# Two gated MLP layers in a one-core Trainium2 kernel: token shift by transfers, 11 column blocks, four banks, bias as a row

## The chip, the core and the metric

The kernel runs on one NeuronCore of one Trainium2 chip. The metric is the device time of one execution in microseconds (us). A core has TensorE (PE in the profile; its weight loads are PEld), VectorE (DVE), ScalarE (ACT), GpSimd (POOL), SyncE (SP, which here only issues transfers) and 16 DMA engines.

## The reference, cut to what matters

The input is x, 4096 tokens of 256 channels. First comes global causal attention with 16 heads, whose result is kept for the end. Then come DEPTH = 2 layers, each a local attention and a gated MLP, and at last a gate that puts the two paths together. The change touches the gated MLP alone:

```python
DIM = 256; HID = int(DIM * 4 * 2 / 3)      # 682
def shift_token(t):                         # half of the channels come from the token before
    t1, t2 = jnp.split(t, 2, axis=-1)
    t2 = jnp.pad(t2, ((0, 0), (1, 0), (0, 0)))[:, :-1]
    return jnp.concatenate([t1, t2], axis=-1)
...
h = shift_token(x)
mu = h.mean(-1, keepdims=True)
var = h.var(-1, keepdims=True)
h = (h - mu) / jnp.sqrt(var + 1e-05) * lg + lb
h = h @ w1 + b1                             # 256 -> 2 * 682
a, g = jnp.split(h, 2, axis=-1)
h = a * jax.nn.gelu(g, approximate=False)
x = x + h @ w2 + b2                         # 682 -> 256
```

## The kernel before, in words

The stages run one after the other with a barrier between them: `project`, `global_attention`, `project_out`, then twice `local_attention_layer` and `mlp_layer`, and `gate`. X, the residual stream, stays on the chip as X[128 tokens, 32 tiles, 256 channels].

`mlp_layer` (L1406) handles the 4096 tokens in NC = 8 chunks of 512 (TPC = 4 tiles of 128). Each float32 product is made of three fp32r ones (`product3`, L72): each operand is split in a high part, rounded, and a low part, the rest. Before the first chunk there is a preparation: SP loads w1 into `stage` (L1468) and six small tensors (L1470); ACT rounds w1 (L1500), DVE subtracts (L1582); then SP loads w2 into the same `stage` (L1474), and ACT and DVE do the same with it. ACT and PE also wait for the small tensors.

Then each engine runs the function `slot(k)` for k = 0 to 8. In slot k the front half works on chunk k (shift, statistics, normalisation, turning) and the back half on chunk c = k - 1 (up projection, gate, down projection). Slot 0 has only a front half, slot 8 only a back half; slots 1 to 7 are iterations of a loop. Within a slot each engine has a fixed order:

- PE: the shift (L1535, L1537), eight matmuls in float32 by a shift matrix and a carry matrix into `bank_sh`; the up projection (L1554 to L1557), 12 column blocks of 128, of which each takes 6 matmuls of 512 columns (two halves of the channels, three products); the turning of the normalised chunk k, 8 transposes (L1563); the down projection (L1572), 72 matmuls of 256 columns into `bank_y`, the first tile of which waits for each split of u in turn (`ul_done`).
- The blocks of the up projection alternate between a gate block (n even) and an up block (n odd) and use UR = 3 banks of PSUM in turn: block n >= 3 waits until the reader of block n - 3 is done (L1549), which is Gelu on ACT (L1514) for a gate block and the product on DVE (L1621) for an up block.
- DVE, all of the front half first: bn_stats of the half of the channels that stays (L1590) and of the shifted half in PSUM (L1593), bn_aggr (L1598), epsilon (L1600), the normalisation in eight pieces (L1604, L1606); then X + b2 into `xb` (L1611); then for each of HC = 6 pairs of blocks the product (up + bias) * gelu (L1621) and its rounding (L1627); then the split of the turned chunk (L1634, L1637); at last X = bank_y + xb (L1645).
- ACT: six Gelu (L1514), then scale and bias of the turned chunk (L1520). POOL: the power -1/2 for the normalisation (L1485), then six low parts of u (L1493).

Three transfers of other stages are read below for their rate: `kst<-gone` (L554) copies 128 runs of 512 B from 128 partitions into 2 partitions, `oraw<-o_raw` (L802) reads an array whose outermost dimension is 4 into 64 partitions, and `y_rows<-oy` (L806) has 128 partitions on both sides. An `xs` transfer of the shifted half is 127 partitions x 4 runs of 512 B.

HID is 682 = 5 * 128 + 42, so that the sixth pair of blocks holds 42 columns of use in each block of 128; the rest are zeros.

Of the kernel before, what the change touches and what calls it, by code (L numbers as in the profile page):

```python
# [41 lines left out]
HP = HC * P  # L42

# [1362 lines left out]
def mlp_layer(nc, layer, X, w_1, w_2, b_1, ln_cols, b_2, ident, shift, carry):  # L1406


    with ExitStack() as ctx:
# [5 lines left out]
        def psum(name, shape):  # L1415
# [5 lines left out]
        b1_sb = sb("b1", [P, 2 * HC])  # L1421
        ln_sb = sb("ln", [P, 2 * EC])
        b2_sb = sb("b2", [P, E])
        id_sb = sb("id", [P, P])
        sh_sb = sb("sh", [P, P])
        ca_sb = sb("ca", [P, P])
        half = sb("half", [P, TPC])
        stats = sb("stats", [P, TPC, 2, 6])
# [10 lines left out]
        xb = sb("xb", [P, TPC, E])  # L1439
        bank_sh = psum("bank_sh", [P, TPC, P])  # L1440
        bank_t = psum("bank_t", [P, EC, C])
        UR = 3
# [5 lines left out]
        names = ("sh", "st", "ag", "ve", "rs", "hn", "th", "hf", "hhi", "hlo", "um", "gl", "uf", "uh", "ul", "y", "xb", "x3")  # L1448
        (sh_done, st_done, ag_done, ve_done, rs_done, hn_done, th_done, hf_done, hhi_done, hlo_done, um_done,
         gl_done, uf_done, uh_done, ul_done, y_done, xb_done, x3_done) = [sem(n) for n in names]  # L1450
# [10 lines left out]
        def tile(k, a):  # L1461
            return X[:, bass.ds(k * TPC + a, 1), :]
# [3 lines left out]
        @block.sync  # L1466
        def _(sp):
            sp.dma_start(stage[:, :], w_1).then_inc(w1_in, 16)  # L1468
            for dst, src in ((b1_sb, b_1), (ln_sb, ln_cols), (b2_sb, b_2), (id_sb, ident), (sh_sb, shift), (ca_sb, carry)):
                sp.dma_start(dst[:, :], src).then_inc(const_in, 16)  # L1470

            sp.wait_ge(wh_done, 1)
            sp.wait_ge(wl_done, 1)
            sp.dma_start(stage[:, 0:HC * E], w_2).then_inc(w2_in, 16)  # L1474

        @block.gpsimd
        def _(pool):
# [3 lines left out]
            def slot(k):  # L1481
                if live(k):
                    pool.wait_ge(ve_done, k + 1)
                    upto(pool, hn_done, 2 * TPC * k)
                    pool.tensor_tensor(rstd[:, :], ve[:, :], half[:, :], ALU.pow).then_inc(rs_done, 1)  # L1485
                if live(k - 1):
                    c = k - 1
                    for m in range(HC):
# [4 lines left out]
                        pool.tensor_tensor(u_lo[:, m, :], uf[:, m % 2, :], u_hi[:, m, :].bitcast(F32), ALU.subtract  # L1493
                                           ).then_inc(ul_done, 1)
            slots(pool, slot)

        @block.scalar
        def _(act):
# [4 lines left out]
            act.wait_ge(const_in, 6 * 16)  # L1503

            def slot(k):
                if live(k - 1):
                    c = k - 1
                    for m in range(HC):
                        act.wait_ge(um_done, 2 * (c * HC + m) + 1)
# [4 lines left out]
                        act.activation(gl[:, m % 2, :], bank_u[(2 * m) % UR][:, :], ACT.Gelu,  # L1514
                                       bias=b1_sb[:, HC + m:HC + m + 1]).then_inc(gl_done, 1)
# [9 lines left out]
        def _(pe):  # L1525
            pe.wait_ge(const_in, 6 * 16)
# [3 lines left out]
            def slot(k):  # L1530
                if live(k):
                    upto(pe, hn_done, 2 * TPC * k)
                    for a in range(TPC):
                        first = isinstance(k, int) and k == 0 and a == 0
                        last = pe.matmul(bank_sh[:, a, :], sh_sb[:, :], tile(k, a)[:, :, P:E], start=True, stop=first)  # L1535
                        if not first:
                            last = pe.matmul(bank_sh[:, a, :], ca_sb[:, :], tile(k, a - 1)[:, :, P:E], start=False, stop=True)  # L1537
                    last.then_inc(sh_done, 1)
                c = k - 1
                if live(c):  # L1540
                    pe.wait_ge(hlo_done, c * EC + EC)
                    pe.wait_ge(hhi_done, c * EC + EC)
                    for m in range(HC):
                        for side in range(2):
                            n = 2 * m + side

                            if n >= UR:
                                mm, ss = (n - UR) // 2, (n - UR) % 2
                                pe.wait_ge(uf_done if ss else gl_done, c * HC + mm + 1)  # L1549
                            elif n == 0:  # L1550
                                upto(pe, uf_done, c * HC)
                                upto(pe, gl_done, c * HC)
                            col = (HP if side == 0 else 0) + m * P
                            for e in range(EC):  # L1554
                                last = product3(pe, bank_u[n % UR][:, :], w1_hi[:, e, col:col + P], w1_lo[:, e, col:col + P],
                                                h_hi[:, e, :], h_lo[:, e, :], e == 0, e == EC - 1)
                            last.then_inc(um_done, 1)  # L1557
                if live(k):
                    pe.wait_ge(hn_done, 2 * TPC * (k + 1))
# [5 lines left out]
                if live(c):  # L1565
                    upto(pe, x3_done, c * TPC)
                    for a in range(TPC):
                        for m in range(HC):
                            if a == 0:
                                pe.wait_ge(ul_done, c * HC + m + 1)  # L1570
                            tok = slice(a * P, (a + 1) * P)
                            last = product3(pe, bank_y[:, a, :], u_hi[:, m, tok], u_lo[:, m, tok], w2_hi[:, m, :],  # L1572
                                            w2_lo[:, m, :], m == 0, m == HC - 1)
# [5 lines left out]
        def _(dve):  # L1579
# [219 lines left out]
```

## Time and profile before

| | |
|---|---|
| median of 3 runs | 3534.86 us (3532.56 to 3538.28) |
| profiled execution: its time / its span | 3537.87 us / 3536.2 us |
| PE busy, share of the span | 3162.5 us, 89% |
| DVE busy | 2373.5 us, 67% |
| ACT busy | 1722.9 us, 49% |
| POOL busy | 785.7 us, 22% |
| mean granted TensorE clock | 0.954 |
| gated layer 0, from the load of w1 to the last X | 2338.4 to 2613.9 us of the span |
| gated layer 1, the last X | 3499.0 us |

Busy shares are averages over stages with different limits. The two gated layers take some 275 us each, and what an edit in them is worth is to be read there, from what each engine waits for in one slot.

### The profile page before, as it was taken

What the parts mean: (1) busy time and instruction counts of PE and PEld (TensorE: products, weight loads), DVE (VectorE), ACT (ScalarE), POOL (GpSimd) and SP (SyncE); (2) the same over time, 40 slices, a digit from 0 to 9 for tenths busy, and PEclk for the clock granted to TensorE, in tenths of its full rate; (3) what the DMA queues carried; (4) which work ended last, traced back from release to release, by engine and by line L of the source; (5) the groups of instructions that cost most, each with busy time, mean ns of one, the idle gap of its engine ahead of it and who ended that gap; (6) DMA issues with size and microseconds to landing.
All of it is one profiled execution on the core that took longest, in us unless ns stands there. A gap on an engine that the chain in (4) does not pass through costs nothing. (4 is left out here: it accounts for less than half of the span.)

```text
span 3536.2 us, 76024 instructions
## 1 busy us (share of the span) xinstructions
PE 3162.5 (89%) x31852; PEld 1928.2 (55%) x31852; DVE 2373.5 (67%) x3284; ACT 1722.9 (49%) x3173; POOL 785.7 (22%) x757
## 2 busy tenths in 40 slices
PE   7799999999999999998689999959968999995995
PEld 6433333344443433343467777647856777764784
DVE  7699998987899988772356555535535655553554
ACT  4267777887678888886033333222213333322221
POOL 7400000000110000001043333312224333331221
PEclk9699999999999999997899999979989999997998
DMA  7420001000210000000300000000010000000004
GB/s 242 130 61 17 9 9 45 9 14 13 59 39 9 13 13 5 5 8 23 127 24 14 20 20 14 8 32 0 0 34 24 14 20 20 14 8 32 0 0 143
DMA packets 62014, 113.62 MB, mean 32 GB/s; under 512 B 9608, under 2 KB 25480, under 8 KB 61192
## 3 DMA queue, kind: packets, MB, share of 16 engines
q1 hardware_dynamic: 57608, 102.84, 9.5%
q10 hardware_dynamic: 4096, 6.30, 0.7%
q8 instruction: 237, 3.88, 0.5%
q14 instruction: 73, 0.60, 0.1%
HBM read 74.77 MB, written 33.55 MB: 31 GB/s over the span
## 5 line engine op out<-in xcount | busy, mean ns | idle before, releaser
L649 DVE TENSOR_REDUCE mp<-ps_m 128x2 f32<-128x1024 f32 (+3 forms) x1152 | 1275.7, 1135 | 186.2 <-PE ps_m L700 132.9
L627 ACT ACTIVATE probs<-ps_s 128x512 f32<-128x512 f32 (+3 forms) x2304 | 1162.6, 561 | 372.8 <-PE ps_s L724 342.2
L740 PE MATMUL ps_o<-probs,vall 128*32 128x256 f32 (+3 forms) x9216 | 708.4, 379 | 15.7 <-POOL probs L604 9.1
L724 PE MATMUL ps_s<-qst,kst 64*128 64x512 f32 (+3 forms) x2304 | 593.0, 484 | 4.5 <-ACT probs L627 3.1
L700 PE MATMUL ps_m<-kst,qst 64*128 64x512 f32 (+3 forms) x2304 | 479.1, 399 | 33.4 <-DVE mp L649 15.8
L724 PEld LDWEIGHTS ps_s<-qst,kst 64*128 64x128 f32 x2304 | 240.7, 186 | 457.2 <-ACT probs L627 399.3
L740 PEld LDWEIGHTS ps_o<-probs,vall 128*32 128x32 f32 x9216 | 185.5, 109 | 339.8 <-issue 175.3
L700 PEld LDWEIGHTS ps_m<-kst,qst 64*128 64x128 f32 x2304 | 231.8, 191 | 78.0 <-DVE mp L649 58.7
L989 POOL TENSOR_TENSOR a_rot<-a_t 128x512 f32<-128x512 f32 x128 | 163.0, 1273 | 448.6 <-DVE a_t L1344 448.6
L1514 ACT ACTIVATE m_gl<-m_bank_u,m_b 128x512 f32<-128x512 f32 x96 | 66.3, 691 | 344.4 <-PE m_bank_u L77 344.4
L1035 ACT ACTIVATE a_sq<-a_BP 128x512 f32<-128x512 f32 x128 | 76.6, 599 | 292.8 <-PE a_BP L77 292.8
L604 POOL TENSOR_SCALAR_AFFINE_SELECT probs<-probs 128x256 f32<-128x256 f32 x256 | 103.2, 408 | 509.0 <-ACT probs L627 508.9
L1344 DVE SCALAR_TENSOR_TENSOR a_t<-a_BP,a_sc,a_tab 128x256 f32<-128x256 f32 x384 | 167.1, 476 | 63.5 <-ACT a_sq L1035 63.0
L593 POOL TENSOR_TENSOR msplit<-negm,mzero 128x16 fp32r<-128x16 f32 x32 | 7.2, 224 | 903.4 <-DVE negm L655 903.4
L995 POOL TENSOR_TENSOR a_rn<-a_ssc,a_half 128x32 f32<-128x32 f32 x32 | 174.1, 5440 | 94.1 <-DVE a_ssc L1401 94.1
L1042 ACT ACTIVATE a_oTh<-a_on 128x512 fp32r<-128x512 f32 x64 | 40.4, 631 | 296.6 <-DVE a_on L1354 296.6
L75 PE MATMUL m_bank_u<-m_hh,m_w1h 128*128 128x512 f32 x384 | 155.6, 405 | 27.8 <-DVE m_uf L1621 27.8
L1350 DVE RECIPROCAL a_rec<-a_B 128x256 f32<-128x256 f32 x64 | 112.3, 1754 | 100.0 <-PE a_B L1213 99.5
L1014 ACT ACTIVATE a_PT<-a_SU 128x1024 f32<-128x1024 f32 (+1 forms) x128 | 122.3, 1007 | 108.9 <-PE a_SU L1135 108.9
L1317 DVE TENSOR_REDUCE a_mx<-a_SU 128x4 f32<-128x1024 f32 (+1 forms) x128 | 148.6, 1203 | 39.1 <-PE a_SU L1111 39.1
L1493 POOL TENSOR_TENSOR m_ul<-m_uf,m_uh 128x512 fp32r<-128x512 f32 x96 | 126.2, 1315 | 193.8 <-DVE m_uh L1627 193.8
L76 PE MATMUL m_bank_u<-m_hl,m_w1h 128*128 128x512 f32 x384 | 152.4, 397 | 0.0
(182 smaller groups left out, 5271.3 us busy)
## 6 DMA issues: line engine op xcount, KB each, us to landing
a_tab<-in_rope SPq DMA_DIRECT2D x32, 512.0 KB
q_parts<-pparts SPq DMA_DIRECT2D x32, 256.0 KB, 3.9
k_parts<-pparts SPq DMA_DIRECT2D x32, 256.0 KB, 3.9
qst<-q_parts SPq DMA_DIRECT2D x64, 128.0 KB, 2.6
o_raw<-o_sb SPq DMA_DIRECT2D x32, 256.0 KB, 2.1
X<-in_x SPq DMA_DIRECT2D x8, 512.0 KB, 6.1
kst<-k_parts SPq DMA_DIRECT2D x32, 128.0 KB, 3.7
qst<-q_parts SPq DMA_DIRECT2D x64, 64.0 KB, 2.6
```

The source lines that it names most:

```text
L75: pe.matmul(out, a_hi, b_hi, start=start, stop=False)
L76: pe.matmul(out, a_hi, b_lo, start=False, stop=False)
L627: act.activation(probs[:, s % PR, h, off:C], sslots[n % SR][:, off:C], ACT.Exp, scale=float(D) ** -0.5).then_inc(exp_done, 1)
L649: dve.tensor_reduce(mp[b % 2][:, h:h + 2, cc:cc + 1], slot[:, :, 0:width], AX.X, ALU.max).then_inc(max_read, 1)
L700: last = pe.matmul(slot[:, x, 0:width], qst[q_slot(b)][rows, hp, a * P:(a + 1) * P], kst[g % 2][rows, hp, cc * C:cc * C + width], start=Tr ...
L724: pe.matmul(sslots[n % SR][:, off:C], kst[g % 2][rows, hp, i * P:(i + 1) * P], qst[q_slot(b)][rows, hp, off:C], start=True, stop=True).the ...
L740: last = pe.matmul(ps_o[32 * h:32 * h + VW, lo:hi], vall[:, i, (g * GH + h) * DV:(g * GH + h) * DV + VW], probs[:, s % PR, h, lo:hi], star ...
L989: pool.tensor_tensor(rot[:, g, :, :].rearrange("p a b -> p (a b)"), t[:, n % 2, 0, :, :].rearrange("p a b -> p (a b)"), t[:, n % 2, 1, :, ...
L995: pool.tensor_tensor(rn[:, :, :, :].rearrange("p a b c -> p (a b c)"), ssc[:, :, :, :].rearrange("p a b c -> p (a b c)"), half[:, :], ALU. ...
L1317: dve.tensor_reduce(mx[:, w % 2, 2 * b:2 * b + 2, :], SU[:, 2 * b:2 * b + 2, :].rearrange("p i (q c) -> p i q c", q=2)[:, :, :, lo:N2], AX ...
L1344: dve.scalar_tensor_tensor(out=dst, in0=src, scalar=s, in1=table, op0=ALU.mult, op1=ALU.mult).then_inc(rope_done, 1)
L1493: pool.tensor_tensor(u_lo[:, m, :], uf[:, m % 2, :], u_hi[:, m, :].bitcast(F32), ALU.subtract).then_inc(ul_done, 1)
```

## The change

- The shift matmuls, their bank, and the two matrices go. SP copies chunk k into a new tile `xs` by three transfers inside SBUF: the half that stays (128 partitions), the shifted half (partitions 0 to 126 to partitions 1 to 127), and row 0 from partition 127 of the tile before. It issues those of chunk 0 between the loads of w1 and of the small tensors, those of chunk k >= 1 when chunk k - 1 is normalised. bn_stats and the normalisation read `xs`, 256 channels at a time.
- The weights w1 are laid out as NB = 11 blocks: gate and up alternate for five pairs, and the last block holds both remainders, up columns in rows 0 to 41 and gate columns in rows 64 to 105. The last Gelu and the last product both wait for it.
- `bank_u` has four banks in place of three.
- b2 becomes row 42 of the last block of w2, against a row of ones in u; `xb` goes, and X = bank_y + X is done in two pieces of 512 in place of four. The last block of the down projection uses 64 rows.
- DVE no longer does the front half ahead of the gate: bn_stats follows the first product, bn_aggr the second, the normalisation the third and the fourth (two tiles each). POOL does the power after its second low part.

```diff
-        UR = 3
+        UR = 4
...
+        def shifted(sp, k):
+            t = k * TPC
+            sp.dma_start(xs[:, :, 0:P], X[:, t:t + TPC, 0:P]).then_inc(xs_in, 16)
+            sp.dma_start(xs[1:P, :, P:E], X[0:P - 1, t:t + TPC, P:E]).then_inc(xs_in, 16)
+            if k == 0:
+                sp.wait_ge(one_set, 1)
+                sp.dma_start(xs[0:1, 1:TPC, P:E], X[P - 1:P, 0:TPC - 1, P:E]).then_inc(xs_in, 16)
+            else:
+                sp.dma_start(xs[0:1, :, P:E], X[P - 1:P, t - 1:t + TPC - 1, P:E]).then_inc(xs_in, 16)
...
             sp.dma_start(stage[:, :], w_1).then_inc(w1_in, 16)
-            for dst, src in ((b1_sb, b_1), (ln_sb, ln_cols), (b2_sb, b_2), (id_sb, ident), (sh_sb, shift), (ca_sb, carry)):
+            shifted(sp, 0)
+            for dst, src in ((b1_sb, b_1), (ln_sb, ln_cols), (id_sb, ident)):
                 sp.dma_start(dst[:, :], src).then_inc(const_in, 16)
 
             sp.wait_ge(wh_done, 1)
             sp.wait_ge(wl_done, 1)
             sp.dma_start(stage[:, 0:HC * E], w_2).then_inc(w2_in, 16)
+
+            for k in range(1, NC):
+                sp.wait_ge(hn_done, TPC * k)
+                shifted(sp, k)
...
+                    if live(k) and m == 1:
+                        pool.wait_ge(ve_done, k + 1)
+                        upto(pool, hn_done, TPC * k)
+                        pool.tensor_tensor(rstd[:, :], ve[:, :], half[:, :], ALU.pow).then_inc(rs_done, 1)
...
+                        n, r = block_of(m, 0), gate_rows(m)
+                        act.activation(gl[uses(m), m % 2, :], bank_u[n % UR][r, :], ACT.Gelu,
+                                       bias=b1_sb[r, n:n + 1]).then_inc(gl_done, 1)
...
-                if live(k):
-                    upto(pe, hn_done, 2 * TPC * k)
-                    for a in range(TPC):
-                        first = isinstance(k, int) and k == 0 and a == 0
-                        last = pe.matmul(bank_sh[:, a, :], sh_sb[:, :], tile(k, a)[:, :, P:E], start=True, stop=first)
-                        if not first:
-                            last = pe.matmul(bank_sh[:, a, :], ca_sb[:, :], tile(k, a - 1)[:, :, P:E], start=False, stop=True)
-                    last.then_inc(sh_done, 1)
...
+                    for n in range(NB):
+                        if n >= UR:
+                            pe.wait_ge(uf_done if n % 2 else gl_done, c * HC + (n - UR) // 2 + 1)
...
+            def gated(c, m):
+                n, r, b = c * HC + m, uses(m), block_of(m, 1)
+                dve.wait_ge(um_done, c * NB + b + 1)
+                dve.wait_ge(gl_done, n + 1)
...
+                dve.scalar_tensor_tensor(out=uf[r, m % 2, :], in0=bank_u[b % UR][r, :], scalar=b1_sb[r, b:b + 1],
+                                         in1=gl[r, m % 2, :], op0=ALU.add, op1=ALU.mult).then_inc(uf_done, 1)
+                dve.wait_ge(uf_done, n + 1)
...
+                dve.tensor_copy(u_hi[r, m, :], uf[r, m % 2, :]).then_inc(uh_done, 1)
+
+            def measure(k):
+                dve.wait_ge(xs_in, 48 * (k + 1))
+                for a in range(TPC):
+                    dve.bn_stats(stats[:, a, :], xs[:, a, :]).then_inc(st_done, 1)
...
+            def normalize(k, a):
+                if a == 0:
+                    dve.wait_ge(rs_done, k + 1)
+                    upto(dve, th_done, k * EC)
+                dve.tensor_scalar(hn[:, a, :], xs[:, a, :], mv[:, a, 0:1], rstd[:, a:a + 1], ALU.subtract, ALU.mult
+                                  ).then_inc(hn_done, 1)
...
+                for m in range(HC):
+                    if live(c):
+                        gated(c, m)
+                    if live(k):
                         if m == 0:
+                            measure(k)
+                        elif m == 1:
+                            aggregate(k)
+                        elif m in (2, 3):
+                            normalize(k, 2 * m - 4)
+                            normalize(k, 2 * m - 3)
...
-                    for a in range(TPC):
-                        dve.tensor_tensor(tile(c, a).rearrange("p a e -> p (a e)"), bank_y[:, a, :], xb[:, a, :], ALU.add
-                                          ).then_inc(x3_done, 1)
+                    for a in range(0, TPC, 2):
+                        x = X[:, bass.ds(c * TPC + a, 2), :]
+                        dve.tensor_tensor(x, bank_y[:, a:a + 2, :], x, ALU.add).then_inc(x3_done, 1)
```

## Rows read from the trace of the kernel before

**Rows 1.** Stretches: us, then each engine's busy time, granted clock, DMA share, GB/s.

```profile
2432.10:2463.00 30.90, 28.48 (x170) 24.62 (x170) 17.61 (x46) 6.88 (x9) 8.91 (x7) 1.00 0.00 0
```

**Rows 2.** Timeline, DVE, X written at a slot's end: start, us, instruction, idle before.

```profile
2401.71 1.42 DVE L1645 TENSOR_TENSOR X<-m_bank_y,m_xb 128x256 f32 x4 [5.34 <-PE m_bank_y L77]
...
2586.32 1.42 DVE L1645 TENSOR_TENSOR X<-m_bank_y,m_xb 128x256 f32 x4 [5.58 <-PE m_bank_y L77]
2612.51 1.42 DVE L1645 TENSOR_TENSOR X<-m_bank_y,m_xb 128x256 f32<-128x256 f32 x4 [8.17 <-PE m_bank_y L77]
...
3285.37 1.42 DVE L1645 TENSOR_TENSOR X<-m_bank_y,m_xb 128x256 f32 x4 [5.58 <-PE m_bank_y L77]
3317.49 1.42 DVE L1645 TENSOR_TENSOR X<-m_bank_y,m_xb 128x256 f32 x4 [5.34 <-PE m_bank_y L77]
```

**Rows 3.** Timeline, PE, one slot of layer 0.

```profile
2432.16 0.38 PE L1535 MATMUL m_bank_sh<-X,m_sh 128*128 x2
...
2433.86 0.48 PE L75 MATMUL m_bank_u<-m_hh,m_w1h 128*128 128x512 f32 x1
...
2439.30 0.40 PE L77 MATMUL m_bank_u<-m_hh,m_w1l 128*128 128x512 f32 x1
2441.76 0.50 PE L75 MATMUL m_bank_u<-m_hh,m_w1h 128*128 128x512 f32 x1 [2.06 <-DVE m_uf L1621]
...
2453.07 1.04 PE L1563 MATMUL m_bank_t<-m_id,m_hn 128*128 128x128 f32 x8
...
2455.59 0.28 PE L77 MATMUL m_bank_y<-m_w2h,m_ul 128*128 128x256 f32 x1
2456.24 0.38 PE L75 MATMUL m_bank_y<-m_w2h,m_uh 128*128 128x256 f32 x1 [0.36 <-POOL m_ul L1493]
```

**Rows 4.** Timeline, DVE, ACT and POOL, the same slot.

```profile
2439.62 1.42 DVE L1611 TENSOR_TENSOR m_xb<-X,m_b 128x256 f32<-128x256 f32 x4
...
2442.86 0.96 DVE L1627 CAST m_uh<-m_uf 128x512 fp32r<-128x512 f32 x1
...
2451.86 0.69 ACT L1514 ACTIVATE m_gl<-m_bank_u,m_b 128x512 f32<-128x512 f32 x1 [2.11 <-PE m_bank_u L77]
...
2453.42 0.75 DVE L1621 SCALAR_TENSOR_TENSOR m_uf<-m_bank_u,m_b,m_gl 128x512 f32<-128x512 f32 x1 [1.59 <-PE m_bank_u L77]
...
2454.72 1.46 POOL L1493 TENSOR_TENSOR m_ul<-m_uf,m_uh 128x512 fp32r<-128x512 f32 x1 [1.52 <-DVE m_uh L1627]
```

**Rows 5.** Timeline, preparation, slot 0 and start of slot 1 of layer 0.

```profile
2351.29 0.33 SPq L1474 DMA_DIRECT2D m_stage<-in_w  x1
2355.76 1.48 ACT L1502 ACTIVATE m_w2h<-m_stage 128x1536 fp32r<-128x1536 f32 x1 [7.93 <-DMA m_stage<-in_w]
...
2362.54 0.89 DVE L1593 BATCH_NORM_STATS2 m_stats<-m_bank_sh 128x6 f32<-128x128 f32 x4 [2.73 <-PE m_bank_sh L1537]
...
2367.74 1.97 PE L1563 MATMUL m_bank_t<-m_id,m_hn 128*128 128x128 f32 x8 [5.24 <-DVE m_hn L1606]
...
2372.78 0.61 PE L75 MATMUL m_bank_u<-m_hh,m_w1h 128*128 128x512 f32 x1
```

**Rows 6.** Timeline, DVE, the first stage: bn_stats of four tiles of 256 channels.

```profile
4.89 1.41 DVE L323 BATCH_NORM_STATS2 pstats<-X 128x6 f32<-128x256 f32 x4 [4.89 <-DMA X<-in_x]
```

**Rows 7.** Stretches, columns as in rows 1: kst<-gone; oraw<-o_raw; a stretch with y_rows<-oy.

```profile
242.00:242.50 0.50, 0.41 (x4) 0.10 (x4) 0.50 (x2) 0.17 (x2) 0.00 (x0) 1.00 0.14 43
1695.00:1705.00 10.00, 10.00 (x40) 7.38 (x39) 4.83 (x8) 0.00 (x0) 0.00 (x0) 1.00 0.26 102
1713.00:1717.00 4.00, 4.00 (x16) 2.85 (x15) 1.56 (x3) 0.00 (x0) 0.00 (x0) 1.00 1.03 413
```

**Rows 8.** Timeline, SP's queue: the issue of the transfer in the first stretch of rows 7.

```profile
240.17 1.14 SPq L554 DMA_DIRECT2D kst<-gone  x2
```

**Rows 9.** DMA issues: tile, queue, count, KB each, median us to landing.

```profile
m_b<-in_b SPq DMA_DIRECT2D x2, 128.0 KB, 5.5
...
obo<-in_b_o SPq DMA_DIRECT2D x1, 128.0 KB, 2.6
```

More of the change, by code:

```diff
@@ L1403, in _, with mlp_layer @@
                 divide(k - 3, 0)
-def mlp_layer(nc, layer, X, w_1, w_2, b_1, ln_cols, b_2, ident, shift, carry):
+def mlp_layer(nc, layer, X, w_1, w_2, b_1, ln_cols, ident):
     with ExitStack() as ctx:
@@ L1481, in slot @@
             def slot(k):
-                if live(k):
[L1483 to L1488, printed above, removed]
+                c = k - 1
+                for m in range(HC):
+                    if live(c):
                         pool.wait_ge(uh_done, c * HC + m + 1)
@@ L1542, in slot @@
                     pe.wait_ge(hhi_done, c * EC + EC)
[L1543 to L1557, printed above, removed]
+                    for n in range(NB):
+                        if n >= UR:
+                            pe.wait_ge(uf_done if n % 2 else gl_done, c * HC + (n - UR) // 2 + 1)
+                        elif n == 0:
+                            upto(pe, uf_done, c * HC)
+                            upto(pe, gl_done, c * HC)
+                        col = slice(n * P, (n + 1) * P)
+                        for e in range(EC):
+                            last = product3(pe, bank_u[n % UR][:, :], w1_hi[:, e, col], w1_lo[:, e, col],
+                                            h_hi[:, e, :], h_lo[:, e, :], e == 0, e == EC - 1)
+                        last.then_inc(um_done, 1)
                 if live(k):
-                    pe.wait_ge(hn_done, 2 * TPC * (k + 1))
+                    pe.wait_ge(hn_done, TPC * (k + 1))
                     upto(pe, hf_done, k * EC)
@@ new lines, in measure, with aggregate @@
+            def measure(k):
+                dve.wait_ge(xs_in, 48 * (k + 1))
+                for a in range(TPC):
+                    dve.bn_stats(stats[:, a, :], xs[:, a, :]).then_inc(st_done, 1)
+            def aggregate(k):
+                dve.wait_ge(st_done, TPC * (k + 1))
+                dve.memset(idle[:, :], 0.0)
+                for a in range(TPC):
+                    dve.bn_aggr(mv[:, a, :], stats[:, a, :]).then_inc(ag_done, 1)
+                dve.wait_ge(ag_done, TPC * (k + 1))
+                dve.tensor_scalar(ve[:, :], mv[:, :, 1], EPS, None, ALU.add).then_inc(ve_done, 1)
@@ L1628, in slot @@
+                for m in range(HC):
+                    if live(c):
+                        gated(c, m)
+                    if live(k):
+                        if m == 0:
+                            measure(k)
[4 more added lines that the diff above has]
+                            normalize(k, 2 * m - 3)
                 if live(k):
@@ L1640, in slot @@
                     dve.wait_ge(y_done, c + 1)
-                    dve.wait_ge(xb_done, TPC * (c + 1))
-                    upto(dve, sh_done, (k + 1) if not isinstance(k, int) else min(k + 1, NC))
-                    for a in range(TPC):
-                        dve.tensor_tensor(tile(c, a).rearrange("p a e -> p (a e)"), bank_y[:, a, :], xb[:, a, :], ALU.add
-                                          ).then_inc(x3_done, 1)
+                    for a in range(0, TPC, 2):
+                        x = X[:, bass.ds(c * TPC + a, 2), :]
+                        dve.tensor_tensor(x, bank_y[:, a:a + 2, :], x, ALU.add).then_inc(x3_done, 1)
             slots(dve, slot)
```

118 lines of the change are left out of this document (49 added, 69 removed).

## The prediction, made before the changed kernel was run

> **What bounds the kernel now.** The change is confined to the two gated layers, so I read a gated slot. The stretches give granted clock 1.00, PE busy 28.5 of 30.9 us and DVE 17.6 [rows 1]: PE bounds it. The writes of X mark the slots: six full slots of layer 0 take (2586.32 - 2401.71) / 6 = 30.77 us each, the last 26.2, slot 1, from the turning at 2367.74 to the write at 2401.71, some 34.0 [rows 2, 5]. PE's timeline divides a slot [rows 3]: shift 2432.16 to 2433.86 = 1.70 us; four blocks in 5.67, of which the last matmul starts at 2439.30; then a hole until 2441.76, which at one matmul each 0.233 us is 2.22 us; eight blocks in 11.3 to 2453.07 (1.40 us a block); turning, 0.8; 15 down matmuls; 2455.59 to 2456.24, where one matmul needs 0.12, is 0.53 lost to the last low part of POOL; the rest of the down projection. The hole is of DVE's order: block 4 waits for the first product, which stands behind the whole front half and `xb` (to 2441.0) [rows 4].
>
> **The change part by part, per steady slot.**
>
> - *Shift matmuls* go: -1.70 [rows 3]. Nothing hides them, PE being the bound.
> - *Eleven blocks for twelve*: one block, -1.40. The down projection stays at 72 matmuls; 64 rows in place of 128 I cost at nothing (bounds 0 and, if a matmul went by its rows, 12 x 0.12 / 2 = -0.7).
> - *The hole*: -2.22. The first product now stands first in its slot. It waits only for block 1, 2.8 us in, and takes 0.75 [rows 4]; block 5 wants its bank at 7.0, block 4 that of the first Gelu, done at about 2.3. The four banks give a block of room more. What is late next is the front half, below.
> - *The last pair*: Gelu of the last block ran beside the last up block; now it follows it. The chain block, (Gelu 0.69), product 0.75, rounding, low part 1.46 [rows 4] grows by Gelu and a handover, 0.69 + 0.05. PE waits there already, so all of it shows: +0.74, and the wait becomes about 1.27. Bounds: 0.5 if the smaller partition count makes something shorter, 1.5 if DVE is late by one piece of normalisation.
> - *The front half in the gaps.* Products come each 2.8 us and need 0.75 + 0.43, so each gap has 1.6. bn_stats of four tiles of 256 took 1.41 [rows 6], bn_aggr and epsilon some 0.8, two normalisations some 0.8: each fits its gap. POOL: the second low part ends 8.3 us in, the power at 9.3, the normalisation starts at 9.8 and ends, undisturbed, at 13.4; the turning wants it at 15.4. Cost 0. If this cover of 2 us is gone, each us late is one us per slot.
> - *DVE and POOL*: a rounding that began while POOL worked took 0.96 in place of 0.43 [rows 4], that is, it waited. The normalisation of tiles 2 and 3 now begins just as POOL begins the fourth low part (1.29); if it waits too, it ends at 14.7, still ahead of 15.4. The Trainium skill (SBUF — State Buffer, "SBUF: two separate sides") says that the loser of the shared port blocks for the whole instruction; by that rule the 14.7 is the figure to hold against the trace, and the sum is the same.
> - *`xb`* goes and the last sum is two pieces for four: DVE has room, and PE's wait for it (`x3_done`) lies a slot away. 0.
> - *SP and the transfers.* SP has nothing else in these layers. The doubtful one is the shifted half: 508 runs of 512 B on 127 partitions. In the rows, two partitions on one side ran at 43 GB/s, an outermost dimension of four at 102, 128 at 413 [rows 7]: 21.5, 25.5 and 25.8 GB/s for each of 2, 4, 16 DMA engines, as if the outermost dimension were dealt out evenly. 127 can't be dealt out evenly but to one. Bounds: 260 KB over 16 engines, under 1 us plus latency; over one, 260 KB / 21.5 = 12.1 us. I take one engine, the nearest rule to the rows. With 2.1 us before the first packet (two issues of about 0.5; the packets of a copy issued at 240.17 fill the stretch from 242.00 [rows 7, 8]) it lands 14.2 us after the last normalisation. That is 13.4 + 14.2 = 27.6; the next slot's bn_stats come at 26.2 + 4.2 = 30.4. Hidden, with 2.8 us to spare, 1.5 if POOL delays the normalisation. The Trainium skill (DMA: Bandwidth & Descriptors, "Why a DMA increments its semaphore by 16 and not by 1") says the same of 127 partitions: one engine.
>
> Per steady slot: -1.70 - 1.40 - 2.22 + 0.74 = -4.58, to 26.2 us. Six per layer: -27.5.
>
> **Preparation and slot 0.** Here the long transfer isn't hidden. It is issued behind w1 and ahead of w2, and a queue's later transfers wait: 128 KB landed 5.5 us after its issue behind w1, 2.6 elsewhere [rows 9]. w1 ends at about 2345; one engine then works 0.8 + 12.1 us on `xs`, to 2357.9, and only then on its sixteenth of w2 (48 KB, 1.9 us): 2359.8 in place of 2355.76 [rows 5], +4.1. Against it: DVE's wait of 2.73 for the shift goes [rows 5], bn_stats take 1.41 where two halves took 1.76, the normalisation four pieces for eight, about -0.75: -3.8. Sum +0.3 a layer. Bounds: -3.8 if 16 engines share it, +1 if w1 suffers too.
>
> **Slot 1.** The blocks began at 2372.78; DVE's split lets them begin 0.5 sooner, but at half clock: the turning at 2367.74 took 1.97 us where a warm one takes 1.04 [rows 3, 5], and the shift matmuls that ran until the clock rose are gone. A matmul of 512 columns at 1.2 GHz is 0.43 for 0.23; some 5 us of it, as long as turning and shift took before the rise, cost 2.3. The first `xs` of the loop lands 14.2 us after the normalisation of chunk 0, bn_stats wait for it (3 us), and the whole front half runs late, so that the last product and the turning just meet it. Blocks end at about 22.2, u is complete at 25.8, the down projection ends at 32.6 us, where it was 33.8: -1.2. Bounds -3.5 and +1.5.
>
> **Slot 8**: one block less, the longer last pair: -1.40 + 0.74 = -0.7.
>
> Per layer 0.3 - 1.2 - 27.5 - 0.7 = -29.1; two layers -58.2. In layer 1 slot 2 took 32.1 in place of 30.8 [rows 2]; the clock fell after a hole of 2 us. With holes of 1.3 I expect it not to: -1.3. Sum **-59.5 us**, against the profiled execution (3537.87, span 3536.2, so 1.7 around it) 3478.4; that execution is 3.0 above the median 3534.86, so **3475 us**.
>
> **The rivals.**
>
> - *A. Sixteen engines share the shifted half.* For it: 512 runs would divide, and no row has 127. Against: rows 7 as read. Then preparation and slot 0 give -3.8 in place of +0.3, slot 1 about -0.2 more: 2 x 4.3 = 8.6, 3467 us.
> - *B. The front half or the last pair is late.* Two registers more to wait for and the lock between DVE and POOL let the turning wait, or u ends a further 1 to 1.5 us late, or the clock falls in the new waits. For it: 0.7 us of cover by the locked figure. 14 slots x 1.3 = +18: 3493 us.
> - *C. Slower than before: the transfer sets the pace.* Then the period is landing time plus the way from bn_stats to the last normalisation (1.4 + 1.2 + POOL's low part and power 2.4, two normalisations, a product, two more: 7.8 us). It decides at 26.2 when landing takes 18.4, and loses to 30.77 at 23, which is 41 ns a run of 512 B for the 23.8 of rows 7. Were it 60 ns, as with crowded engines, the landing is 32.6, the period 40.4: 14 x 9.6 + preparation 2 x 18 = +170, some 3705 us. Against: in these stretches DMA share is 0.00 [rows 1], nothing crowds it.
> - *D. The change doesn't do what it says*: the banks or the order don't free block 4, the hole stays, 14 x 2.2 back: 3506 us.
>
> **How the numbers follow.** A measurement of this kernel tells about 0.2% (7 us) from no change. Forecast 0.6, A 0.16, B 0.13, C 0.05, D 0.04, and 0.02 for a mixture of B and C that ends within 7 us of before. Forecast, A, B and D are faster by more than that, C is slower. The range takes in A below, with slot 1 at its good end, and B above with the upper bound of the last pair: 3460 to 3500. Faster 0.93, same 0.02, slower 0.05.
>
> **What would show it.** In the changed profile: no L75 matmul of block 4 idle behind a product; slots of 26.2 us; PE idle some 1.0 to 1.3 before the sixth split of u; a gap between the loads of w2 and its rounding of 8.5 us in place of 4.5; bn_stats waiting for `xs` in slot 1 only; the first blocks of slot 1 at half clock. Wrong if: slots are equal to landing time plus 8 (C); w2 lands in 4.5 us (A); the turning waits for DVE in each slot (B).

## The result, and the profile after

| | us, median (lowest to highest) | ratio to before, 95% interval |
|---|---|---|
| before | 3535.69 (3531.43 to 3541.13), 6 runs | |
| after | 3520.51 (3511.63 to 3522.59), 6 runs | 0.9954 [0.994, 0.9968] |

Faster by 15 us (0.5%) where 60 were forecast, and outside the range of 3460 to 3500. The profiled execution took 3522.59, with a span of 3520.9.

So that noise elsewhere in the kernel stays out, I cut each gated layer by its own marks, the issue of w1, the turning of chunk 0, and the writes of X, and add the two layers. Forecast is the row of before with the prediction's terms.

| both gated layers, us | before | forecast | after |
|---|---|---|---|
| w1's issue to the turning | 58.4 | 59.0 | 62.6 |
| slot 1, from the turning | 68.2 | 65.8 | 82.9 |
| slots 2 to 7 | 370.4 | 314.1 | 331.8 |
| slot 8 | 52.6 | 51.2 | 55.5 |
| sum | 549.6 | 490.1 | 532.8 |

The rest of the kernel took 2986.6 and 2988.1. Of the 42.7 us that are missing, 17.1 lie in slot 1, 17.7 in the slots that repeat, 3.6 in the preparation and 4.3 in slot 8. The slots that repeat come first. In the timeline of VectorE of the kernel after, the writes of X at the ends of slots 2, 3 and 4 of layer 0 (against [rows 2]):

```profile
2440.83 1.29 DVE L1666 TENSOR_TENSOR X<-m_bank_y,X 128x512 f32 x2 [6.84 <-PE m_bank_y L79]
2468.10 1.29 DVE L1666 TENSOR_TENSOR X<-m_bank_y,X 128x512 f32 x2 [6.85 <-PE m_bank_y L79]
2499.98 1.29 DVE L1666 TENSOR_TENSOR X<-m_bank_y,X 128x512 f32 x2 [12.44 <-PE m_bank_y L79]
```

A slot takes 27.27 us, not 26.2, and one, slot 4, takes 31.88. The timeline of TensorE in the down projection of such a slot (against [rows 3]); columns are start, duration, instruction, idle before:

```profile
2456.11 1.04 PE L1572 MATMUL m_bank_t<-m_id,m_hn 128*128 128x128 f32 x8
...
2458.63 0.28 PE L79 MATMUL m_bank_y<-m_w2h,m_ul 128*128 128x256 f32 x1
2459.82 0.38 PE L77 MATMUL m_bank_y<-m_w2h,m_uh 64*128 64x256 f32 x1 [0.91 <-POOL m_ul L1509]
...
2467.11 0.28 PE L79 MATMUL m_bank_y<-m_w2h,m_ul 128*128 128x256 f32 x1
2467.32 0.38 PE L77 MATMUL m_bank_y<-m_w2h,m_uh 64*128 64x256 f32 x1
2467.55 0.28 PE L78 MATMUL m_bank_y<-m_w2l,m_uh 64*128 64x256 f32 x1
2467.66 0.27 PE L79 MATMUL m_bank_y<-m_w2h,m_ul 64*128 64x256 f32 x1
2467.86 0.50 PE L77 MATMUL m_bank_u<-m_hh,m_w1h 128*128 128x512 f32 x1
```

The wait for the last low part is 1.19 - 0.12 = 1.07 us, where I had 1.27. But the first matmul after a change of row count starts 0.21 us after its predecessor, and the next 0.23 after it, where 0.12 is the usual spacing in these rows. From 2467.11 to 2467.66 the three steps take 0.55 for 0.36: 0.19 us lost at each change, and a slot has eight changes. The weight loads of the same moment show how:

```profile
2466.88 0.19 PEld L78 LDWEIGHTS m_bank_y<-m_w2l,m_uh 128*128 128x128 f32 x1
2467.00 0.19 PEld L79 LDWEIGHTS m_bank_y<-m_w2h,m_ul 128*128 128x128 f32 x1
2467.32 0.18 PEld L77 LDWEIGHTS m_bank_y<-m_w2h,m_uh 64*128 64x128 f32 x1
```

The load for the matmul at 2467.11 begins 0.11 us ahead of it, at 2467.00. The one at the change begins together with its matmul, at 2467.32: it isn't pulled ahead of the running matmul.

The shifted half, in stretches of slot 1 and of a steady slot (the last three columns are granted clock, DMA share, GB/s; against [rows 7]), and in the timelines of SP's queue, ScalarE and VectorE:

```profile
2378.00:2386.00 8.00, 8.00 (x30) 6.29 (x30) 1.18 (x2) 3.34 (x4) 1.29 (x1) 0.81 0.08 20
2432.00:2440.00 8.00, 7.44 (x54) 6.71 (x54) 1.99 (x3) 0.00 (x0) 0.50 (x1) 1.00 0.08 20
```

```profile
2339.19 0.33 SPq L1482 DMA_DIRECT2D m_stage<-in_w  x1
...
2341.14 15.72 SPq L1465 DMA_DIRECT2D m_xs<-X  x1
...
2358.37 0.36 SPq L1489 DMA_DIRECT2D m_stage<-in_w  x1
```

```profile
2362.80 1.48 ACT L1522 ACTIVATE m_w2h<-m_stage 128x1536 fp32r<-128x1536 f32 x1 [14.19 <-DMA m_stage<-in_w]
```

```profile
2388.39 1.41 DVE L1621 BATCH_NORM_STATS2 m_stats<-m_xs 128x6 f32<-128x256 f32 x4 [6.09 <-DMA m_xs<-X]
```

One engine it is, at 19 to 20 GB/s: the packets in the trace start 27 ns apart (37 in a microsecond), for the 23.8 ns a run of [rows 7]. Each takes 34 ns, so they overlap a little, and the share is 0.08 in place of one sixteenth. What I hadn't seen is SP: the issue of the next transfer took 15.72 us in place of some 0.7, so SP stood until the one engine had drained most of its 508 runs (in slot 1, some 390 of them when the issue ended), and everything behind it in SP's program, w2 among them, was issued late. w2 goes out 19.2 us after w1, where it was 12.9 (w1 at 2338.38 in the trace of before, w2 in [rows 5]). In slot 1 of layer 0, bn_stats begin 17.8 us after the last normalisation (2370.58), not 14.2.

Last, POOL's low part of the last pair: once in an ordinary slot, once in the slot of 31.88. VectorE's split stands beside each, and the granted clock behind the second.

```profile
2458.38 1.39 POOL L1509 TENSOR_TENSOR m_ul<-m_uf,m_uh 42x512 fp32r<-42x512 f32 x1 [0.46 <-DVE m_uh L1616]
2485.76 2.91 POOL L1509 TENSOR_TENSOR m_ul<-m_uf,m_uh 42x512 fp32r<-42x512 f32 x1 [0.36 <-DVE m_uh L1616]
```

```profile
2458.22 1.82 DVE L1657 CAST m_hh<-m_hf 128x512 fp32r<-128x512 f32 x2
...
2485.60 0.74 DVE L1657 CAST m_hh<-m_hf 128x512 fp32r<-128x512 f32 x2
2486.27 1.28 DVE L1660 TENSOR_TENSOR m_hl<-m_hf,m_hh 128x512 fp32r<-128x512 f32 x2
```

```profile
2488.72 0.38 PE L77 MATMUL m_bank_y<-m_w2h,m_uh 64*128 64x256 f32 x1 [2.53 <-POOL m_ul L1509]
```

```profile
2490.00:2497.00 7.00, 7.00 (x33) 6.33 (x31) 0.00 (x0) 0.00 (x0) 0.00 (x0) 0.52 0.08 19
```

In the slot of 31.88 VectorE began its split 0.16 us ahead of POOL, and POOL's instruction took 2.91 us in place of 1.39. TensorE waited 2.53 us for it, and then worked at 1.2 GHz (granted clock 0.52) for 7 us. In the ordinary slot VectorE's two roundings took 1.82 us beside POOL in place of 0.74. The Trainium skill (SBUF — State Buffer, "SBUF: two separate sides") has the shared port as a lock: whoever starts first keeps it for the whole instruction, and the other blocks. That one blocks the other agrees with both rows. But POOL's 1.52 us more are longer than any one of VectorE's four instructions, of 0.4 to 0.7 us: 1.39 us before POOL's end is 2487.28, near the end of their whole run at 2487.55.

### The profile page after: what moved, and what is told of

Same layout as the page of the kernel before. It is cut to its first block and busy times, and to the rows that moved or that the text cites. A ratio compares the mean times of both kernels' runs of the same rounds, so it can differ in the third digit from the quotient of the medians.

```text
span 3520.9 us, 74950 instructions
## 1 busy us (share of the span) xinstructions
PE 3141.2 (89%) x31504; PEld 1895.6 (54%) x31504; DVE 2356.4 (67%) x3070; ACT 1722.6 (49%) x3173; POOL 789.0 (22%) x757
## 5 line engine op out<-in xcount | busy, mean ns | idle before, releaser
L77 PE MATMUL m_bank_u<-m_hh,m_w1h 128*128 128x512 f32 x352 | 144.4, 410 | 11.1 <-DVE m_uf L1611 5.7
L77 PE MATMUL a_BP<-a_hTh,a_wqh 128*128 128x256 f32 x512 | 149.0, 291 | 1.8 <-DVE a_t L1346 1.8
```

What stands on the lines that cost most here:

```text
L77: pe.matmul(out, a_hi, b_hi, start=start, stop=False)
```

## The experiments

**Theory.** Three costs of the change, none of them in the sum: (1) the one-engine transfer holds SP and is late in slot 1; (2) TensorE pays for each change between 128 and 64 rows; (3) POOL's last low part loses the port to VectorE's split. Rivals: the gap is in the new order of VectorE's work, or in too few banks. In the expectations below, "slots" are the times between writes of X. Every kernel is the kernel after with the edit named, except e8 and e11, which start from the kernel before.

**e1_split.** The shifted half in two transfers, 112 and 15 partitions (VectorE waits for one more).

```diff
-            sp.dma_start(xs[1:P, :, P:E], X[0:P - 1, t:t + TPC, P:E]).then_inc(xs_in, 16)
+            sp.dma_start(xs[1:113, :, P:E], X[0:112, t:t + TPC, P:E]).then_inc(xs_in, 16)
+            sp.dma_start(xs[113:P, :, P:E], X[112:P - 1, t:t + TPC, P:E]).then_inc(xs_in, 16)
```

> The changed kernel with one edit: the shifted half goes as 112 partitions and 15 partitions in place of 127. Theory L (127 partitions run on one DMA engine; that one transfer makes SP stand in its issues, delays w2, and makes bn_stats of slot 1 late, after which PE idles and its clock falls): w2 issued about 13 us after w1 in place of 19, so the preparation shorter by about 5 to 6 us a layer; bn_stats of slot 1 no longer wait for xs (6.1 and 6.6 us now), block 7 doesn't stall (3 us) and the half clock after it goes: slot 1 shorter by 5 to 8 us a layer. Together 20 to 28 us less than the changed kernel, about 3495 us, ratio to the kernel before about 0.988. Steady slots stay at 27.26 us. Rival R (the time went into the half-array matmuls and the last low part alone, the transfer is hidden): no change, ratio 0.995, slot 1 still over 40 us.

3489.99 us (3485.98 to 3506.44), ratio 0.9862 [0.9837, 0.9887]. The profiled execution is the slowest of them. Steady slots take 27.28, as in the kernel after, so the transfer was hidden there. From w1 to the turning 51.3 us for both layers (after: 62.6; before: 58.4), slot 1 69.7 (82.9). SP's queue in e1_split:

```profile
2344.65 0.33 SPq L1483 DMA_DIRECT2D m_stage<-in_w  x1
...
2346.75 0.95 SPq L1463 DMA_DIRECT2D m_xs<-X  x1
...
2358.16 0.33 SPq L1490 DMA_DIRECT2D m_stage<-in_w  x1
```

No issue stands now, and w2 goes out 13.5 us after w1. The median is 5 us below the 3495 expected, preparation and slot 1 gave what the theory said, and this is cause 1. Slot 8 got longer, 30.0 us in both layers (after: 27.0 and 28.5), as the granted clock fell there (0.58 and 0.57 over 6.6 us); the last section comes back to it.

**e2_rows.** All 128 rows in the last block of the down projection; rows 64 to 127 of u are set to 0 once, the weights there are 0.

```diff
-                            r = slice(0, P) if m < HC - 1 else slice(0, P // 2)
-                            last = product3(pe, bank_y[:, a, :], u_hi[r, m, tok], ...
+                            last = product3(pe, bank_y[:, a, :], u_hi[:, m, tok], ...
```

> The changed kernel with one edit: the last block of the down projection takes all 128 rows (rows 64 to 127 set to zero once). Theory S (each switch between 128-row and 64-row matmuls costs PE 0.1 to 0.2 us, 8 switches a slot): steady slots fall from 27.26 to 26.1 to 26.2 us, 16 slots x 1.1 = 18 us less than the changed kernel, about 3502 us, ratio 0.990. The matmuls after a change of rows are again 0.12 us apart. Rival (the excess over 26.2 is only the longer last pair): no change, 27.26 us, ratio 0.995.

3511.74 us (3505.69 to 3513.01), ratio 0.9925 [0.9899, 0.9952], where 3502 was expected: half of the gain is missing. Half of the slots take 25.9 to 26.0 us: the cost of the changes is real, -1.3 a slot. The others take 28.5 to 31.4. The chain in slot 2 of layer 0, from the timelines of VectorE and TensorE of e2_rows:

```profile
2412.93 1.41 DVE L1623 BATCH_NORM_STATS2 m_stats<-m_xs 128x6 f32<-128x256 f32 x4 [1.51 <-DMA m_xs<-X]
```

```profile
2422.67 1.09 PE L1572 MATMUL m_bank_t<-m_id,m_hn 128*128 128x128 f32 x8 [0.57 <-DVE m_hn L1637]
2428.36 0.58 PE L77 MATMUL m_bank_y<-m_w2h,m_uh 128*128 128x256 f32 x1 [2.65 <-POOL m_ul L1509]
```

With slots of 26 us the transfer isn't hidden any more; the normalisation is late, the turning waits, and the split then falls in front of POOL's last low part. This happened in six of the twelve steady slots (TensorE's wait 2.65 us each). Causes 1 and 3 eat what 2 gives.

**e3_tail.** VectorE makes the sixth low part itself, right behind its rounding; POOL has only five.

```diff
+                if m == HC - 1:
+                    dve.wait_ge(uh_done, n + 1)
+                    dve.tensor_tensor(u_lo[r, m, :], uf[r, m % 2, :], u_hi[r, m, :].bitcast(F32), ALU.subtract
+                                      ).then_inc(ll_done, 1)
```

> The changed kernel with one edit: DVE makes the sixth low part of u itself, right after its rounding; POOL makes five. Theory P (the last low part on POOL either takes 1.39 us or, where DVE's split of the turned chunk gets the shared port first, 2.91 us; then PE idles 2.5 us and its clock falls for some 5 us): the steady slot falls by 0.6 to 0.8 us, as 0.65 us of DVE takes the place of 1.39 plus a handover, and no slot of 31.9 us is left. 16 x 0.7 + 5 to 8 = 16 to 19 us less than the changed kernel, about 3503 us, ratio 0.991. Rival (the port isn't the cause of the 2.91 us; DVE is the one that is late): no gain, or DVE's part waits for POOL's fifth low part and the slot stays at 27.2.

3511.69 us (3508.12 to 3514.49), ratio 0.9926 [0.9901, 0.9951]. No steady slot is over 28 us, as cause 3 wants it. By itself that is weak, since the kernel after had only one such slot in twelve; the six of e2 say more. The rest of the expectation, 0.6 to 0.8 us less a slot and 3503, was missed: slots take 27.3 to 27.5 us in layer 0 and 27.1 to 27.3 in layer 1, since what is saved is waited for elsewhere (the waits of e3_tail from 2410 to 2610 us; columns are total us, times, longest):

```profile
DVE m_stats L1629 <- DMA m_xs<-X: 6.3, 6, 1.1
...
PE m_bank_y L77 <- DVE m_ul L1623: 3.2, 7, 0.9
PE m_bank_t L1572 <- DVE m_hn L1643: 1.8, 6, 0.4
```

In each of these slots bn_stats wait for the transfer and the turning waits for the normalisation: the transfer sets the pace, rival C's mechanism, at 27.4 us in layer 0. That is 17.8 us from the last normalisation to bn_stats and 9.6 from there to the last normalisation again.

**e4_split_rows.** e1 and e2 together.

> The edits of e1 and e2 together. If L and S are independent: the sum, 38 to 46 us less than the changed kernel, about 3478 us, ratio 0.984, which is the forecast on record. If one covers the other: less than 30 us.

3466.84 us (3461.34 to 3467.66), ratio 0.9798 [0.9773, 0.9824]. All steady slots take 25.9 to 26.0. Against the kernel after, 31 us came from e1, 9 from e2, and 54 from both; in the gated layers alone 24.4, 8.2 and 52.7. Neither expectation (the sum of the two, or less than 30) foresaw this: each edit alone leaves the other's limit in place, and together they give more than their sum.

**e5_all_three.** e4 with e3's low part.

> The shifted half as 112 and 15 partitions, all 128 rows in the last down block, and the last low part made by VectorE (the three changes of e1_split, e2_rows and e3_tail together). Theory (PE sets the slot, and the last low part stands on its path; in e3_tail nothing came of it because the transfer was late): slots go from 25.95 to about 25.2 us, 16 slots less 0.7 = -11 us against the 3466.8 of e4_split_rows, about 3456, ratio to the kernel before 0.977. Rival (VectorE is the next thing late: in its gaps stands the front half, and 0.5 us more of work there pushes the normalisation behind the turning): slots stay at 25.9 or grow, 3465 to 3480, ratio 0.980 to 0.984, with waits of the turning for the normalised tokens.

3451.63 us (3444.05 to 3454.33), ratio 0.9765 [0.9744, 0.9786]. Slots take 25.23, as the theory had it, and with e12 below this is the fastest version of the study. What e5 gains over e4 isn't the port: in e4 TensorE waits 0.9 us for the last low part in every steady slot, so POOL never lost it there. It is the shorter last low part (the wait is 0.23 in e5), which pays once the transfer is out of the way.

**e6_banks3, e7_front_first, e9_front_banks3.** e4 with three banks; e4 with VectorE's front half ahead of its first product again, and POOL's power first; and both.

```diff
-        UR = 4
+        UR = 3
...
-                            pe.wait_ge(uf_done if n % 2 else gl_done, c * HC + (n - UR) // 2 + 1)
+                            pe.wait_ge(uf_done if (n - UR) % 2 else gl_done, c * HC + (n - UR) // 2 + 1)
```

```diff
-                for m in range(HC):
-                    if live(c):
+                if live(k):
+                    measure(k)
+                    aggregate(k)
+                    for a in range(TPC):
+                        normalize(k, a)
+                if live(c):
+                    for m in range(HC):
```

> e4_split_rows with three banks in place of four for the up blocks. Theory (the order of VectorE's work alone closes the hole; the fourth bank gives nothing): slots 25.9 to 26.0, 3467 +-3, ratio 0.980. Rival (the four banks are needed): block 3 waits for the first product and each later block for one product more, 0.5 to 2 us a slot, 14 slots, 3474 to 3495, ratio 0.982 to 0.988.

> e4_split_rows with VectorE's whole front half ahead of the first product, as in the kernel before, and the power first on POOL; four banks kept. Theory (the hole was of the order; four banks hide a part): the first product ends some 7.5 us into the slot where block 5 wants its bank at 7.0 and block 4 that of the first Gelu; 0.5 to 1 us a slot, 14 slots, 3474 to 3481, ratio 0.982 to 0.984. Rival 1 (the order matters in full): the hole of 2.2 us is back, 3498, ratio 0.989. Rival 2 (the banks did it all): 3467, ratio 0.980.

> e4_split_rows with both undone: front half ahead of the first product (as in e7_front_first) and three banks (as in e6_banks3). Each alone cost nothing in the slots. In e7_front_first the first product ended 6.9 us into the slot, and block 5 wanted its bank at 7.0. Theory (either of the two hides the front half, neither is needed once the other is there): with three banks block 4 waits for that product, 5.6 us in, a hole of 1.3 us plus the restart; slots 27.2 to 27.5, 14 slots, about 3487, ratio 0.986. Rival (the hole went with the shift matmuls and the sum of X and bias, neither order nor banks matter): slots 25.9, ratio 0.980 to 0.982.

| | us | ratio, interval | steady slot | both layers |
|---|---|---|---|---|
| e4 | 3466.84 | 0.9798 [0.9773, 0.9824] | 25.93 | 480.1 |
| e6 | 3471.88 | 0.9818 [0.9795, 0.984] | 25.92 | 478.9 |
| e7 | 3462.49 | 0.979 [0.9768, 0.9812] | 25.94 | 479.8 |
| e9 | 3482.93 | 0.983 [0.9811, 0.9849] | 27.34 | 495.8 |

The medians of e4, e6 and e7 differ, but the gated layers don't; what differs lies outside (2984.5 to 2991.3 us in the profiled executions). e7 misses my expectation: I had a hole of 0.5 to 1 us. The front half without the shift's pieces and without `xb` is shorter, its first product ends 6.9 us into the slot, and the bank is wanted at 7.0. In e9 block 4 wants it at 5.6:

```profile
2433.08 0.50 PE L77 MATMUL m_bank_u<-m_hh,m_w1h 128*128 128x512 f32 x1 [1.16 <-DVE m_uf L1614]
```

That wait and the restart make 1.40 a slot. So the order or the fourth bank, either one alone, closes what is left of the hole once the shift matmuls and `xb` are gone.

**e8_before_order, e11_order_late_sum.** The kernel before, with only the new order (front half in the gaps, the power after POOL's second low part); `xb` after the fifth product in e8, after the last split of h in e11.

```diff
+                for m in range(HC):
+                    if live(c):
+                        gated(c, m)
+                    if live(k) and m == 0:
...
+                    if live(c) and m == 4:
...
+                            dve.tensor_tensor(xb[:, a, :], tile(c, a).rearrange("p a e -> p (a e)"), b2_sb[:, :], ALU.add
```

> The kernel before with only the order of VectorE's and POOL's work changed: front half in the gaps between products, the sum of X and the output bias after the fifth product. Three banks, shift by matmuls and twelve blocks stay. Theory (the hole of 2.2 us a slot is of the order): slots of 30.77 us become 28.5 to 28.8, -2.2 x 14 = -31, about 3505, ratio 0.991. Rival (the hole closes only with the fourth bank): slots stay at 30.7, ratio 0.999 to 1.001. Second rival (the normalisation, with its tokens read out of the banks of the shift, becomes late): part of the gain, 3515 to 3530.

> e8_before_order with the sum of X and the output bias moved from after the fifth product to after the last split of h, where VectorE has 5.6 us free. Theory (in e8_before_order the hole went, 2.2 us, and the sum's 2.5 us ahead of the last product gave 1.5 back at the last low part, in each second slot 1.5 more): slots of 28.5 to 28.8, about 3505, ratio 0.991 to 0.992. Rival (the last low part is late for another reason): slots stay at 30.0 to 31.5, ratio 1.000.

e8: 3532.71 us (3525.4 to 3540.44), ratio 1.0004 [0.9992, 1.0017], a miss: slots of 29.8 to 30.0 and of 31.4 to 31.6. No block waits for a bank, so the hole is gone, but it is paid at the other end, by a wait of 1.8 us for the last low part in place of 0.36. VectorE and TensorE of e8, and stretches behind this wait in a slot of 30.02 and in one of 31.55:

```profile
2444.50 2.50 DVE L1634 TENSOR_TENSOR m_xb<-X,m_b 128x256 f32<-128x256 f32 x4
2446.93 0.74 DVE L1593 SCALAR_TENSOR_TENSOR m_uf<-m_bank_u,m_b,m_gl 128x512 f32<-128x512 f32 x1
```

```profile
2449.64 0.39 PE L75 MATMUL m_bank_y<-m_w2h,m_uh 128*128 128x256 f32 x1 [1.82 <-POOL m_ul L1488]
```

```profile
2450.00:2454.00 4.00, 4.00 (x37) 4.00 (x36) 1.07 (x2) 0.00 (x0) 0.00 (x0) 1.00 0.00 0
2480.00:2484.00 4.00, 4.00 (x24) 4.00 (x23) 1.10 (x2) 0.00 (x0) 0.00 (x0) 0.57 0.00 0
```

The wait is the same in both; in the longer slot the granted clock fell behind it.

e11: 3507.46 us (3506.23 to 3509.09), ratio 0.9905 [0.9889, 0.9922]. All steady slots take 28.3, that is -2.46 for the -2.22 forecast. The order is worth what I gave it, if no other work stands ahead of the last product; that `xb` goes was one of the conditions.

**e10_pairs.** e1 with the 64-row block last for tokens 0 and 2, first for tokens 1 and 3: four changes of row count in place of eight.

```diff
-                        for m in range(HC):
+                        order = list(range(HC)) if a % 2 == 0 else [HC - 1] + list(range(HC - 1))
+                        for m in order:
```

> e1_split with the 64-row block last for tokens 0 and 2 and first for tokens 1 and 3 of a slot, so that TensorE changes between 128 and 64 rows four times a slot in place of eight; the same 72 matmuls. Theory (each change costs some 0.15 to 0.19 us): slots go from 27.27 to 26.6, half of the 1.34 between e1_split and e4_split_rows. Rival (a 64-row matmul is slower by itself): slots stay at 27.3. Second rival (only the way in, or only the way out, costs, or the start of an accumulation in 64 rows does): a rise or another share, to be read from the starts of the matmuls.

3474.86 us (3468.14 to 3479.28), ratio 0.9807 [0.9788, 0.9826]. Slots 26.51: -0.77 for four changes, 0.19 each. Two 64-row blocks in a row, in e10's timeline of TensorE:

```profile
2447.85 0.38 PE L77 MATMUL m_bank_y<-m_w2h,m_uh 64*128 64x256 f32 x1
...
2448.19 0.27 PE L79 MATMUL m_bank_y<-m_w2h,m_ul 64*128 64x256 f32 x1
2448.31 0.28 PE L77 MATMUL m_bank_y<-m_w2h,m_uh 64*128 64x256 f32 x1
...
2448.75 0.39 PE L77 MATMUL m_bank_y<-m_w2h,m_uh 128*128 128x256 f32 x1
```

64-row matmuls keep the spacing of 0.12; only the changes cost, in and out. Of the four that are left, one comes right after the wait for the last low part, and e10 to e4 gives 0.58, three times 0.19.

**e12_125.** e5 with the shifted half as 125 and 2 partitions.

> e5_all_three with the shifted half cut as 125 and 2 partitions in place of 112 and 15. Theory (the outermost dimension is dealt evenly to the largest number of engines up to 16 that divides it: 127 to one, 125 to five): 500 runs of 27 ns over five engines, 2.7 us at a DMA share near 0.31 and 95 GB/s; hidden, slots stay 25.23, ratio 0.976 to 0.978. Rival (127 was a case by itself, other counts spread over all 16): share near 1.0 for under 1 us. Second rival (any count that 16 does not divide goes to one engine): 13.6 us at a share of 0.06 to 0.08, slots of 26 and more, ratio 0.982 to 0.987.

3458.12 us (3451.65 to 3464.31), ratio 0.9765 [0.9743, 0.9786]; slots 25.23 to 25.33. Two stretches of one microsecond in the transfer, in a steady slot:

```profile
2414.00:2415.00 1.00, 0.80 (x7) 0.60 (x6) 0.97 (x3) 0.44 (x1) 0.00 (x0) 1.00 0.31 74
2415.00:2416.00 1.00, 0.94 (x7) 0.94 (x8) 1.00 (x4) 0.00 (x0) 0.00 (x0) 1.00 0.35 99
```

And the issue behind it in SP's queue during the preparation:

```profile
2342.03 4.43 SPq L1463 DMA_DIRECT2D m_xs<-X  x1
```

One engine had 0.08 and 19 GB/s. Here the last 500 runs pass in 3.0 us, where one engine would need 13.5: five engines, 30 ns a run for each, and not one or sixteen. In the preparation, where w1 goes ahead in the same queue, SP stands 4.43 us behind them; in a steady slot the same issue takes 0.81. The Trainium skill (DMA: Bandwidth & Descriptors, "Why a DMA increments its semaphore by 16 and not by 1") takes the largest number up to 16 that divides the slowest dimension; 127 to one and 125 to five agree.

## Why the prediction was wrong

- *Eleven blocks, shift, order, last pair: right.* e4 has slots of 25.93 where before had 30.77, -4.84. e11 gives -2.46 for the order; the rest, -2.38, is -1.70 - 1.40 + 0.74 = -2.36 by the prediction's own terms, though no run separates these three. The sum per slot was -4.58.
- *"64 rows in place of 128 I cost at nothing": wrong.* I asked what a 64-row matmul costs and not what it costs to go from one row count to another. It is +1.33 a slot (seven of eight changes show, the first lies behind the wait for the last low part), 16 us in 12 slots, and some 2.7 more in the two slots 8. In the slots that repeat, these 16 and the 4.6 of slot 4, less 2.9 (12 x 0.24) by which the other terms gave more than I had forecast, are the 17.7 missing. My bounds for it, 0 and -0.7, didn't reach above nothing.
- *"SP has nothing else in these layers": wrong where it mattered.* I priced w2 as queued behind the one engine's share, and had it land 4.1 us late. It was issued late: its rounding began 23.6 us after w1's issue, where it was 17.4 [rows 5], 6.2 more. The other side of that step (-3.8) was right: from w2 to the turning 11.98 became 7.93. A layer's preparation came to +2.1 for +0.3. Rival A's price for it, -3.8, is what e1 measured, -3.6 a layer. The sign that I had named for A, a gap of 4.5 us between the issue of w2 and its rounding where one engine would give 8.5, came true at 4.43 with one engine at work: SP was held, so the queue was free by the time w2 was issued.
- *"It lands 14.2 us after the last normalisation ... hidden, with 2.8 us to spare": 17.6 to 17.8, and nothing to spare.* 508 runs at 27 ns are 13.7 for my 12.1, and the row-0 transfer, whose issue in slot 1 lasted until 2384.5, lands behind them. The normalisation ended 14.8 us into the slot, the 14.7 of the port's rule, and not 13.4. With both, my 2.8 us to spare are gone: bn_stats waited 0.21 in an ordinary slot. It stayed hidden only because cause 2 had made the slots longer. In rival C, too, the way from bn_stats to the last normalisation was mis-sized: it counts one product where three stand in that way, and measures 9.6 us, not 7.8. So the transfer decides at 26.2 from a landing of 16.6 on, not of 18.4, and at 17.6 to 17.8 the forecast slot of 26.2 was out of reach whatever the rows cost.
- *Slot 1, -1.2 forecast: +7.3 on average.* I had bn_stats wait 3 us. In layer 0 they waited 6.09, the next product, which stands behind them, was late in freeing a bank (TensorE idle 2.50, then half clock until 2394.7), and the late split took the port from POOL's last low part (idle 2.66, half clock again). In layer 1 the first two waits were 6.63 and 3.17, and the port wasn't lost. e1 takes 6.6 us a layer of this back.
- *Last pair, +0.74: right as a rule, and a race at times.* The size holds (wait 1.07). In slot 4 and slot 1 of layer 0 the port went the other way, and the clock fell: some 4.6 us in slot 4. Rival B named the lock and the clock, at 1.3 us in each slot; it came in some slots, and dearer.

So the order of size was lost in two terms that I took as settled, one at nothing and one as hidden, while the sum of the terms with rows behind them holds to 0.3 us a slot.

## What to carry over

A transfer whose outermost dimension has no divisor near 16 costs more than its own time: look at the issue time of the next transfer on its queue, and cut it into a part that divides and a rest. Count changes of row count between matmuls, not rows; either pad to full height or put the short ones together. When two edits seem to bring little, try them together before judging either: here 31 and 9 made 54, because each had covered the other's wait.

## What the runs showed that I had not expected

- A change between 128 and 64 rows costs 0.19 us each way, and the weight load isn't pulled ahead across it. The Trainium skill (TensorE: Matmul & The Clock Gate, "Step-by-step: what each phase is for") says that a load is pulled ahead when its row group doesn't conflict with the running matmul's, or when it goes to the background weight buffer. That doesn't settle the case: loads from 128 rows to 128 share all their rows and are pulled ahead all the same, and only the change is not. Why, no run here shows.
- SP stands in the issue of a transfer behind a one-engine transfer of 508 runs: 12.4 to 12.5 us in the slots, 15.4 and 15.7 in the preparations, where w1 goes ahead. Behind one of five engines it is 4.43 in the preparation and 0.81 in a slot; behind the 112 partitions of e1 it is 0.95 even in the preparation.
- The clock after a wait. In slot 8 TensorE waits 1.5 us for the last low part, and behind it the granted clock falls in some kernels and layers and not in others. The stretches behind this wait: e10 in layer 0 and in layer 1, then e4 in layer 0.

```profile
2577.00:2582.00 5.00, 5.00 (x30) 4.87 (x29) 0.00 (x0) 0.00 (x0) 0.00 (x0) 0.66 0.00 0
3433.00:3438.00 5.00, 5.00 (x41) 4.73 (x40) 0.00 (x0) 0.00 (x0) 0.00 (x0) 1.00 0.00 0
```

```profile
2570.00:2575.00 5.00, 4.80 (x41) 4.60 (x39) 0.16 (x1) 0.00 (x0) 0.00 (x0) 1.00 0.00 0
```

The slot takes 27.8 us in layer 0 of e10, 26.3 in its layer 1, with the same code and the same wait of 1.50, and 25.7 in e4. Where the last block has 64 rows (after, e1, e10) the clock fell in four of six such slots; where it has 128 (e2, e4, e6, e7, e9) in none of ten. But in e8, all of 128 rows, it fell in some slots behind a wait of 1.8 us. So changes of rows behind the wait go together with the fall, but they don't suffice for it, and behind a somewhat longer wait they aren't needed. What decides stays open.
